# Expert numbers of the passes: packed two to a word and loaded into TensorE's registers in three loads during the routing

## The chip, the cores and the metric

One Trainium2 chip, one core, 8192 tokens of 128 floats. The time is device microseconds of one execution, and runs are compared by their median. Engines: PE is TensorE (PEld its weight loads), DVE VectorE, ACT ScalarE, POOL GpSimd, SP SyncE. Each runs its own stream of instructions, and semaphores order them.

## The reference

```
x = x + cross_attention_ffn(layernorm(x), ctx)      # BitNet linears, 2 attention layers, FFN
tokens = layernorm(x)                               # 8192 x 128
logits = tokens @ router_w.T;  top1 = argmax, p = max softmax      # 8 experts
order  = tokens of one expert by falling p; the first 1280 stay, the others go to expert 0
for e in range(8):  h = relu(tokens @ W1[e] + b1[e]);  y = h @ W2[e] + b2[e]
out = x + y of the token's own expert
```

## The kernel before, in words

The first stages compute the cross attention and its FFN for all tokens, write `x` and its norm's two numbers to rows in DRAM, and form the router's logits. None of that is touched by the change.

**Routing.** DVE and ACT find each expert's threshold digit by digit, and TensorE sums their counts. Beside this DVE builds tables: 8192 tokens sorted by expert are 64 tiles of 128 slots, and as an expert may begin inside a tile, there are `PASSES` = 71 passes, each one tile with one expert. A matmul with a matrix of ones (L1165) spreads four numbers per pass over the partitions of `psum` bank 7. DVE copies two of them as integers to one partition: `expert_of` (L1719) and `slot_of` (L1721). The semaphore `s_seg` (named segments_then_pass_tables_ready) counts these steps: 3 after `expert_of`, 4 after `slot_of`. Then TensorE ranks the tokens (L1178 to L1182), runs twelve matmuls whose result nobody reads (`keep_busy`, L963), and multiplies one-hot tables (L1189): first the 8 first tiles (`place` of `first_tile`, 64 matmuls of 16 columns), then the other 56. DVE makes these tables (L1800: rows; L1777, L1782: tiles), waits in `source(1)` (L1788) for the first product, and writes from it `src_of`, the row numbers of the tokens in each tile.

**The pass loop.** POOL gathers the rows of a tile with an indirect DMA (L640), and scatters finished tiles to the output with another (L647). In POOL's order the gathers of tiles 0 to 30 come first, then gather and scatter alternate for 33 tiles, then the last 31 scatters follow. DVE normalises a gathered tile (L1830), TensorE turns it (L1213), ACT copies it out (L872), TensorE does layer 1 (L1220, four float32 matmuls that run as eight), ACT takes the relu (L884), TensorE does layer 2 (L1229, four again), DVE adds bias and residual (L1836, L1842). SP copies the pass's layer-1 weights into one of seven buffers (L503). TensorE's order for pass a is: turn rows of a+2, layer 1 of a, layer 2 of a-2. Layer 2 addresses the resident second weights by the expert's number, in a register:

```
e = pe.value_load(expert_of[0:1, a:a + 1], min_val=0, max_val=NX - 1)
pe.wait_ge(s_hc, a + 1)
```

Of the kernel before, what the change touches and what calls it, by code (L numbers as in the profile page):

```python
# [9 lines left out]
I32 = mybir.dt.int32  # L10
I16 = mybir.dt.int16
ALU = mybir.AluOpType
# [3 lines left out]
P = 128  # L16
# [8 lines left out]
NX = 8  # L25
# [7 lines left out]
CAP = int(np.ceil(T / NX * 1.25))  # L33
TILES = T // P
PASSES = TILES + NX - 1
RING = 32
TURNS = 8
DEPTH = 4
AHEAD = 7
WP = FF + NC + E  # L40
LAG = RING - 1
FIRST = 8
# [71 lines left out]
def xattn_moe(nc, x, ctx_in, weights, biases, router_w, W1, b1, W2, b2, out):  # L114
    rows = nc.dram_tensor("token_rows", (T, XW), F32).ap()
    with ExitStack() as stack:
        def sb(name, shape, dtype=F32):
            return stack.enter_context(nc.sbuf_tensor(name, shape, dtype))
# [7 lines left out]
        ident = sb("ident", [P, P])  # L126
        ident_b = sb("ident_b", [P, P], BF16)
        ones = sb("ones", [P, P])
# [12 lines left out]
        part_no = sb("part_no", [P, 1])  # L141
# [25 lines left out]
        big = sb("big", [P, T])  # L167
# [70 lines left out]
        hT = [take_f(FF) for _ in range(DEPTH)]  # L238
        w_now = [feat[:, n * WP:(n + 1) * WP] for n in range(AHEAD)]
        src_of = sb("src_of", [P, TILES], I32)  # L240
        expert_of = sb("expert_of", [1, PASSES], I32)
        slot_of = sb("slot_of", [1, PASSES], I32)
        in_pass = sb("in_pass", [P, PASSES])
        spans = sb("spans", [P, 3, NX])
# [3 lines left out]
        by_span = sb("by_span", [P, 3, NX - 1])  # L248
        of_pass = sb("of_pass", [P, 7])
        in_low = sb("in_low", [P, PASSES])  # L250
        by_pass = big[:, 12 * 512:12 * 512 + 4 * PASSES].rearrange("p (k a) -> p k a", a=PASSES)
        cnt = sb("cnt", [P, WAYS - 1])
        reached = sb("reached", [P, WAYS - 1])
        thr_row = sb("thr_row", [NX, NX])
# [6 lines left out]
        n8 = [sb(f"n8_{n}", [P, NX]) for n in range(5)]  # L261
# [113 lines left out]
        s_seg = sem("segments_then_pass_tables_ready")  # L375
# [29 lines left out]
        def bank(n, width=512, rows_=P):  # L405
            return psum[0:rows_, n, 0:width]
# [492 lines left out]
        def _(pe):  # L899
# [60 lines left out]
            def keep_busy(n, columns):  # L960

                for _ in range(n):
                    pe.matmul(columns, f1T[:, 0, 0:P], f1T[:, 0, 0:columns.shape[-1]], start=True, stop=True)  # L963
# [120 lines left out]
            for k, (i, pair) in enumerate(pieces):  # L1084
# [4 lines left out]
                first = 4 * (i % 2) + 2 * pair  # L1089
# [70 lines left out]
            for k in range(LEVELS):  # L1160
                count_up(k, RADIX[k] - 1)
                if k + 1 < len(cuts):
                    tiles_before(cuts[k], cuts[k + 1])
            pe.wait_ge(s_seg, 2)
            pe.matmul(bank(7, 4 * PASSES), ones[:, :], by_pass.rearrange("p k a -> p (k a)"), start=True, stop=True  # L1165
                      ).then_inc(s_tab_mm, 1)
            keep_busy(3, bank(6))
            count_up(LEVELS, 4)
# [11 lines left out]
            pe.wait_ge(s_ms, 2)  # L1180
            pe.matmul(by_tile, ones_b[:, :], above_b.rearrange("p (t e) -> p t e", e=NX), start=False, stop=True)
            pe.matmul(bank(6), not_before_b[:, :], above_b, start=False, stop=True).then_inc(s_ps, 1)  # L1182
            keep_busy(12, bank(4))

            def place(dst, tiles, first, end):
# [17 lines left out]
            m.then_inc(s_inv_mm, 1)  # L1203

            pe.wait_ge(s_seg, 4)
            pe.wait_ge(s_idx, 2)
            pe.wait_ge(s_moe, 16 * 10)

# [12 lines left out]
                m.then_inc(s_l1, 1)  # L1222

            def layer2(a):
                e = pe.value_load(expert_of[0:1, a:a + 1], min_val=0, max_val=NX - 1)
                pe.wait_ge(s_hc, a + 1)
                wait(pe, s_yt, a - 1)
                for c in range(NC):
                    m = pe.matmul(bank(4 + a % 2, E), hT[a % DEPTH][:, P * c:P * c + P],  # L1229
                                  w2s[:, bass.ds(e, 1), c, :].rearrange("p e d -> p (e d)"),  # L1230
                                  start=(c == 0), stop=(c == NC - 1))
                m.then_inc(s_l2, 1)
# [13 lines left out]
        def _(dve):  # L1246
            ch = Chain(dve, s_dve)

            def do(ins):
                ch.link(ins)  # L1250
                ch.join()
# [262 lines left out]
            for k, (i, pair) in enumerate(pieces):  # L1514
                if by_vector(k):
                    dve.wait_ge(s_h, k + 1)
                    first = 4 * (i % 2) + 2 * pair
# [116 lines left out]
                                         accum_out=cnt[:, column:column + 1])  # L1634

            first, start, end = spans[:, 0, :], spans[:, 1, :], spans[:, 2, :]
            spread = bank(7, 4 * PASSES).rearrange("p (k a) -> p k a", a=PASSES)

            def pass_tables(k):

                tokens, kept, dropped, kept_to, dropped_to = (n[:, :] for n in n8)
                upto, lowest, highest, tiles_of = (n[:, :] for n in n8[0:4])
                if k == 0:
                    dve.wait_ge(s_rs_pe, 1)
                    do(dve.tensor_reduce(tokens, bank(6).rearrange("p (t e) -> p e t", e=NX), AX, ALU.add))
                elif k == 1:
                    do(dve.tensor_scalar(kept, tokens, float(CAP), None, ALU.min))
                    ch.link(dve.tensor_tensor(dropped, tokens, kept, ALU.subtract))
                    do(dve.tensor_tensor_scan(kept_to, ones[:, 0:NX], kept, 0.0, ALU.mult, ALU.add))
                elif k == 2:  # L1650
                    do(dve.tensor_tensor_scan(dropped_to, ones[:, 0:NX], dropped, 0.0, ALU.mult, ALU.add))
                    ch.link(dve.tensor_scalar(end, kept_to, dropped_to[:, NX - 1:NX], None, ALU.add))
                    ch.link(dve.tensor_scalar(start[:, 1:NX], kept_to[:, 0:NX - 1], dropped_to[:, NX - 1:NX], None,
                                              ALU.add))
                    ch.join()
                    dve.scalar_tensor_tensor(drop8[:, :], dropped_to, kept[:, 0:1], dropped, ALU.add, ALU.subtract
                                             ).then_inc(s_seg, 1)
                elif k == 3:
                    dve.wait_ge(s_seg, 1)
                    ch.link(dve.tensor_scalar(lowest, start, 0.5 - P / 2, 1.0 / P, ALU.add, ALU.mult))  # L1660
                    ch.link(dve.tensor_scalar(highest, end, P / 2 - 0.5, 1.0 / P, ALU.add, ALU.mult))
                    ch.join()
                    ch.link(dve.tensor_scalar(lowest, lowest, MAGIC, MAGIC, ALU.add, ALU.subtract))
                    do(dve.tensor_scalar(highest, highest, MAGIC, MAGIC, ALU.add, ALU.subtract))
                elif k == 4:
                    do(dve.tensor_tensor(tiles_of, highest, lowest, ALU.subtract))
                    do(dve.tensor_tensor_scan(upto, ones[:, 0:NX], tiles_of, 0.0, ALU.mult, ALU.add))
                    do(dve.tensor_tensor(first, highest, upto, ALU.subtract))
                elif k == 5:
                    ch.link(dve.tensor_tensor(span_steps[:, :, :], spans[:, :, 1:NX], spans[:, :, 0:NX - 1],  # L1670
                                              ALU.subtract))
                    do(dve.tensor_scalar(passed[:, :], upto[:, 0:NX - 1], part_no[:, :], None, ALU.is_le, ALU.add,
                                         accum_out=of_pass[:, 0:1]))
                    do(dve.tensor_tensor(by_span[:, :, :], span_steps[:, :, :],
                                         passed[:, :].unsqueeze(1).to_broadcast([P, 3, NX - 1]), ALU.mult))
                elif k == 6:
                    do(dve.tensor_reduce(span_of[:, :], by_span[:, :, :], AX, ALU.add))
                    do(dve.tensor_scalar(of_pass[:, 4:5], span_of[:, 0:1], part_no[:, :], None, ALU.add))
                    ch.link(dve.scalar_tensor_tensor(of_pass[:, 2:4], of_pass[:, 4:5].to_broadcast([P, 2]), -float(P),
                                                     span_of[:, 1:3], ALU.mult, ALU.add))  # L1680
                elif k == 7:
                    do(dve.tensor_scalar(of_pass[:, 5:6], of_pass[:, 4:5], float(TILES - 1), None, ALU.min))
                    do(dve.tensor_scalar(of_pass[:, 6:7], of_pass[:, 5:6], float(RING), -float(RING), ALU.is_ge, ALU.mult))
                    do(dve.tensor_tensor(of_pass[:, 1:2], of_pass[:, 5:6], of_pass[:, 6:7], ALU.add))
                elif k == 8:
                    dve.tensor_tensor(by_pass, ident[:, 0:PASSES].unsqueeze(1).to_broadcast([P, 4, PASSES]),
                                      of_pass[:, 0:4].unsqueeze(2).to_broadcast([P, 4, PASSES]), ALU.mult
                                      ).then_inc(s_seg, 1)

            def level(k):  # L1690
# [27 lines left out]
            dve.wait_ge(s_tab_mm, 1)  # L1718
            dve.tensor_copy(expert_of[:, :], spread[0:1, 0, :]).then_inc(s_seg, 1)  # L1719
            dve.wait_ge(s_seg, 3)  # L1720
            dve.tensor_copy(slot_of[:, :], spread[0:1, 1, :]).then_inc(s_seg, 1)  # L1721
            dve.wait_ge(s_cnt2, LEVELS + 1)
            do(dve.tensor_scalar(reached[:, 0:4], bank(1 + LEVELS % 2, 4), 0.0, None, ALU.is_ge, ALU.add,
                                 accum_out=met[:, :]))
# [87 lines left out]
            def masks():  # L1812

                ch.link(dve.tensor_tensor(n8[3][:, 0:1], part_no[:, :], end[:, 0:1], ALU.subtract))
                do(dve.tensor_scalar(in_low[:, :], spread[:, 2, :], part_no[:, :], None, ALU.is_le))
                do(dve.scalar_tensor_tensor(in_pass[:, :], spread[:, 3, :], n8[3][:, 0:1], in_low[:, :],
                                            ALU.is_gt, ALU.mult))
            where = {}

# [61 lines left out]
```

## Time and profile before

| | us |
|---|---|
| median of 3 runs | 526.41 |
| lowest, highest | 525.75, 530.26 |
| the profiled execution: its own time, which is its span | 597.2 |
| PE busy, PEld busy in it | 427.6, 348.4 |
| DVE, ACT, POOL busy in it | 368.8, 350.1, 211.0 |

The profiled execution is 70.8 us longer than the median. Its routing begins near 290 us, its first gather stands at 354.47 us, and its last scatter at 590.63 us. In rows of the timeline a start in us, a duration in us, the engine, line and operation, tiles written and read, the count, and in brackets the idle time before and what ended it. Engine names with a q at the end are sequencers.

### The profile page before, as it was taken

The page shows a single profiled execution, that of the slowest core. Times are in us where ns is not written, and L with a number is a line of the kernel's source. Part 1 is how long each engine was busy: PE and PEld are TensorE (multiplying, and loading weights), DVE is VectorE, ACT ScalarE, POOL GpSimd, SP SyncE. Part 2 cuts the span into 40 slices and gives each one's busy share as a digit, 9 for nine tenths or more (in the row PEclk, how much of TensorE's full clock was granted, in tenths as well). Part 3 has the DMA queues.
Part 4 walks back from the last instruction along what each step waited for, and adds up shares of the span by engine and source line. Part 5 has one row for each costly group of instructions (what it writes and reads, how often), then busy time and mean ns, then how long its engine had stood idle before and what let it go on. Part 6 is the DMA issues. An engine that isn't in the chain of part 4 may idle for free.

```text
span 597.2 us, 10833 instructions
## 1 busy us (share of the span) xinstructions
PE 427.6 (72%) x3058; PEld 348.4 (58%) x3058; DVE 368.8 (62%) x957; ACT 350.1 (59%) x805; POOL 211.0 (35%) x296
## 2 busy tenths in 40 slices
PE   0451348999997896898869747229777567789994
PEld 0310135898996342698537346229667566679994
DVE  3999995688887897589998893014222232334442
ACT  0679986788884795987155222126444444457762
POOL 6200571353452000001010527731555555544443
PEclk9999999999999798789775566759887988889998
DMA  9900000000000000024791312223433333445540
GB/s 197 269 20 0 1 0 2 1 2 0 0 0 2 1 1 0 1 54 92 163 261 39 132 33 49 54 74 152 141 129 125 131 124 135 143 152 189 198 165 32
DMA packets 45138, 48.69 MB, mean 82 GB/s; under 512 B 10232, under 2 KB 32800, under 8 KB 45088
## 3 DMA queue, kind: packets, MB, share of 16 engines
q1 hardware_dynamic: 39728, 38.59, 21.4%
q0 software_dynamic: 4096, 8.46, 5.4%
q10 hardware_dynamic: 1264, 1.03, 0.7%
q8 instruction: 24, 0.39, 0.3%
q14 instruction: 26, 0.21, 0.1%
HBM read 16.20 MB, written 8.45 MB: 41 GB/s over the span
## 4 chain that ended last, share of the span: by engine, by line
PE 40%; DVE 23%; ACT 12%; another core or an unknown queue 11%; issue 7%; DVEq 2%; POOL 2%; DMA 2%; SPq 0%; POOLq 0%; ACTq 0%
PE psum L1229 7%; PE psum L1220 6%; PE psum L1012 5%; PE psum L1028 4%; ACT xqT L812 2%; PE psum L1020 2%; POOL out L647 2%; DVE xqT L1830 2%; DMA keys<-in_ctx 2%; DVE xqT L1836 2%; ACT big L715 2%; DVE tok_b L1430 2%; DVE part L1404 1%; ACT tok_b L812 1%
## 5 line engine op out<-in xcount | busy, mean ns | idle before, releaser
L884 ACT ACTIVATE xqT<-psum,feat 128x128 f32<-128x128 f32 x284 | 81.2, 372 | 62.1 <-remote 30.2
L1836 DVE TENSOR_TENSOR xqT<-psum,feat 128x128 f32<-128x128 f32 x71 | 20.7, 292 | 139.8 <-remote 69.5
L647 POOL DMA_INDIRECT out<-xall,src_of x64 | 62.6, 978 | 87.1 <-DVE xall L1842 81.0
L1220 PE MATMUL psum<-xqT,feat 128*128 128x128 f32 x568 | 86.4, 302 | 9.0 <-issue 9.0
L1220 PEld LDWEIGHTS psum<-xqT,feat 128*128 128x128 f32 x568 | 80.2, 218 | 9.2 <-issue 9.2
L1229 PE MATMUL psum<-keys,xqT 128*128 x568 | 84.0, 296 | 1.0 <-issue 0.9
L1229 PEld LDWEIGHTS psum<-keys,xqT 128*128 128x128 f32 x568 | 76.2, 209 | 2.2 <-issue 0.7
L640 POOL DMA_INDIRECT xall<-token_rows,src_of x64 | 62.5, 977 | 38.5 <-issue 18.6
L1213 PE MATMUL psum<-ident,xqT 128*128 128x128 f32 x71 | 22.8, 322 | 53.8 <-DVE xqT L1830 53.3
L872 ACT COPY xqT<-psum 128x128 f32<-128x128 f32 x71 | 19.5, 275 | 58.0 <-remote 46.6
L1213 PEld LDWEIGHTS psum<-ident,xqT 128*128 128x128 f32 x71 | 11.0, 155 | 59.7 <-DVE xqT L1830 56.7
L574 POOL TENSOR_TENSOR qb<-qb,arec 128x308 f32<-128x308 f32 x32 | 21.8, 700 | 64.5 <-DVE arec L1462 64.5
L1028 PE MATMUL psum<-probT,keys 78*128 78x128 f32 x256 | 34.4, 280 | 1.8 <-ACT probT L777 1.8
L594 POOL IOTA tok_b<- 128x2048 bf16 x1 | 2.5, 2470 | 90.9 <-DVE qb L1546 90.9
L963 PE MATMUL psum<-f1T 128*128 128x512 bf16 x99 | 33.8, 493 | 0.0
L1028 PEld LDWEIGHTS psum<-probT,keys 78*128 78x128 f32 x256 | 31.3, 191 | 3.4 <-ACT probT L777 2.7
L1012 PE MATMUL psum<-keys 128*128 128x77 f32 x256 | 32.1, 277 | 1.3 <-ACT keys L662 0.9
L1012 PEld LDWEIGHTS psum<-keys 128*128 128x128 f32 x256 | 30.0, 191 | 4.3 <-ACT keys L662 1.6
L1842 DVE SCALAR_TENSOR_TENSOR xall<-xqT,in_pass,xall 128x128 f32 x71 | 25.0, 352 | 11.4 <-DVE xqT L1836 9.7
L906 PE MATMUL psum<-ident,amax 128*1 128x128 f32 x6 | 2.2, 372 | 39.9 <-DVE amax L1304 15.5
L777 ACT COPY probT<-psum 77x512 f32<-77x512 f32 x32 | 18.3, 576 | 21.0 <-PE psum L1020 21.0
L662 ACT ACTIVATE keys<-psum,bcol,scale 128x308 f32<-128x308 f32 (+1 forms) x48 | 28.3, 658 | 3.1 <-PE psum L988 2.9
(334 smaller groups left out, 1000.6 us busy)
## 6 DMA issues: line engine op xcount, KB each, us to landing
feat<-keys SPq DMA_DIRECT2D x71, 322.0 KB
token_rows<-xall SPq DMA_DIRECT2D x4, 1040.0 KB, 8.5
xall<-in_x SPq DMA_DIRECT2D x8, 512.0 KB, 7.1
keys<-in_L_ffn_W SPq DMA_DIRECT2D x1, 2048.0 KB, 14.1
keys<-in_L_ffn_W SPq DMA_DIRECT2D x8, 256.0 KB, 5.8
keys<-in_ctx SPq DMA_DIRECT2D x4, 462.0 KB, 7.3
xall<-token_rows,src_of POOLq DMA_INDIRECT x64
out<-xall,src_of POOLq DMA_INDIRECT x64
```

The source lines that it names most:

```text
L640: pool.indirect_dma_start(xring[:, t % RING, :], None, rows, bass.IndirectOffsetOnAxis(ap=src_of[:, t:t + 1], axis=0)).then_inc(s_g[t % TU ...
L647: pool.indirect_dma_start(out_rows, bass.IndirectOffsetOnAxis(ap=src_of[:, t:t + 1], axis=0), yring[:, t % RING, :], None).then_inc(s_o[t ...
L662: return act.activation(dst, src_bank, ACT.Identity, bias=bcol[:, b:b + 1], scale=scale[:, k:k + 1])
L884: m = act.activation(hT[a % DEPTH][:, P * c:P * c + P], bank(2 + a % 2)[:, P * c:P * c + P], ACT.Relu, bias=w_now[a % AHEAD][:, FF + c:FF ...
L963: pe.matmul(columns, f1T[:, 0, 0:P], f1T[:, 0, 0:columns.shape[-1]], start=True, stop=True)
L1012: m = pe.matmul(bank(1 + l)[:, CT * b:CT * b + CT], src[n % GR][:, P * b:P * b + P], kT[l][n % GR][:, CT * b:CT * b + CT], start=True, sto ...
L1028: m = pe.matmul(bank(5 + l)[:, P * b:P * b + P], ktok[l][n % (GR if l else 2)][:, P * b:P * b + P], probT[l][:, P * b:P * b + P], start=Tr ...
L1213: pe.transpose(bank(a % 2, P), gn[a % DEPTH], ident[:, :]).then_inc(s_gt, 1)
L1220: m = pe.matmul(bank(2 + a % 2)[:, P * c:P * c + P], w_now[a % AHEAD][:, P * c:P * c + P], gT[a % DEPTH], start=True, stop=True)
L1229: m = pe.matmul(bank(4 + a % 2, E), hT[a % DEPTH][:, P * c:P * c + P], w2s[:, bass.ds(e, 1), c, :].rearrange("p e d -> p (e d)"), start=(c ...
L1836: dve.tensor_tensor(yt[a % 2], bank(4 + a % 2, E), w_now[a % AHEAD][:, FF + NC:WP], ALU.add).then_inc(s_yt, 1)
L1842: dve.scalar_tensor_tensor(y, yt[a % 2], in_pass[:, a:a + 1], y, ALU.mult, ALU.add).then_inc(s_y, 1)
```

## The change

The number of passes is rounded up to 72 (`2 * PAIRS`). After `slot_of` DVE makes a third table, `pair_of`: 36 words, each 8 times the expert of an odd pass plus the expert of the even pass before it.
```diff
+PAIRS = (PASSES + 1) // 2
...
-        expert_of = sb("expert_of", [1, PASSES], I32)
+        expert_of = sb("expert_of", [1, 2 * PAIRS], I32)
+        pair_of = sb("pair_of", [1, PAIRS], I32)
...
-        by_pass = big[:, 12 * 512:12 * 512 + 4 * PASSES].rearrange("p (k a) -> p k a", a=PASSES)
+        by_pass = big[:, 12 * 512:12 * 512 + 4 * 2 * PAIRS].rearrange("p (k a) -> p k a", a=2 * PAIRS)
...
-            pe.matmul(bank(7, 4 * PASSES), ones[:, :], by_pass.rearrange("p k a -> p (k a)"), start=True, stop=True
+            pe.matmul(bank(7, 4 * 2 * PAIRS), ones[:, :], by_pass.rearrange("p k a -> p (k a)"), start=True, stop=True
...
             pe.matmul(bank(6), not_before_b[:, :], above_b, start=False, stop=True).then_inc(s_ps, 1)
+            pe.wait_ge(s_seg, 5)
+            words = []
+            for first in range(0, PAIRS, 12):
+                words.extend(nc.values_load_multi_w_load_instructions(
+                    pair_of[0:1, first:first + 12], engines=(mybir.EngineType.PE,), min_val=0, max_val=NX * NX - 1)[1])
             keep_busy(12, bank(4))
...
-            pe.wait_ge(s_seg, 4)
...
             def layer2(a):
-                e = pe.value_load(expert_of[0:1, a:a + 1], min_val=0, max_val=NX - 1)
+                e = words[a // 2] // NX if a % 2 else words[a // 2] % NX
...
-            dve.tensor_copy(slot_of[:, :], spread[0:1, 1, :]).then_inc(s_seg, 1)
+            dve.tensor_copy(slot_of[:, :], spread[0:1, 1, 0:PASSES]).then_inc(s_seg, 1)
+            dve.wait_ge(s_seg, 4)
+            dve.scalar_tensor_tensor(pair_of[:, :], spread[0:1, 0, 1::2], float(NX), expert_of[:, 0::2],
+                                     ALU.mult, ALU.add).then_inc(s_seg, 1)
...
```

TensorE in the routing, before: the last ranking matmuls, the twelve `keep_busy` matmuls (they read `f1T`) and the first of the products with the one-hot rows in `xqT`.

```order
L1181 MATMUL psum<-tok_b,ones_b 128x64x8 [waits masks_ready]
L1182 MATMUL psum<-tok_b,not_before_b 128x512
L963 MATMUL psum<-f1T 128x512 x12
L1189 MATMUL psum<-big,xqT 128x16 [waits one_hot_rows_ready,tiles_by_partition_ready,one_hot_tiles_then_tiles_by_column_ready]
L1189 MATMUL psum<-big,xqT 128x16 x15
```

The same place in the changed kernel (its lines are 2 to 7 further on; "ISA" are the register instructions and reports).

```order
L1183 MATMUL psum<-tok_b,ones_b 128x64x8 [waits masks_ready]
L1184 MATMUL psum<-tok_b,not_before_b 128x512
L1188 TENSOR_LOAD pair_of [waits segments_then_pass_tables_ready]
L1188 ISA x24
L1188 TENSOR_LOAD pair_of
L1188 ISA x24
L1188 TENSOR_LOAD pair_of
L1188 ISA x24
L965 MATMUL psum<-f1T 128x512 x12
L1196 MATMUL psum<-big,xqT 128x16 [waits one_hot_rows_ready,tiles_by_partition_ready,one_hot_tiles_then_tiles_by_column_ready]
```

Three loads and 72 register instructions now stand between the ranking and the `keep_busy` matmuls.

TensorE in the pass loop, one pass before (the layer-1 matmuls, the load, layer 2; the ISA row ahead of each layer-2 matmul works out its address):

```order
L1220 MATMUL psum<-xqT,feat 128x128 [waits hidden_relu,expert_loaded4,gatheredT_copied]
L1220 MATMUL psum<-xqT,feat 128x128 x3
L1225 TENSOR_LOAD expert_of
L1225 ISA x2
L1229 ISA [waits layer2_biased,hidden_relu]
L1229 MATMUL psum<-keys,xqT 128x128
```

The same pass in the changed kernel:

```order
L1226 MATMUL psum<-xqT,feat 128x128 [waits hidden_relu,expert_loaded4,gatheredT_copied]
L1226 MATMUL psum<-xqT,feat 128x128 x3
L1235 ISA [waits layer2_biased,hidden_relu]
L1235 MATMUL psum<-keys,xqT 128x128
```

The load and its two register instructions are gone from all 71 passes; the first address instruction of a pass holds one more operation, the remainder or quotient.

## Rows read from the trace of the kernel before

**Rows 1.** The page: engines' busy time over the whole span.
```profile
PE 427.6 (72%) x3058; PEld 348.4 (58%) x3058; DVE 368.8 (62%) x957; ACT 350.1 (59%) x805; POOL 211.0 (35%) x296
```
**Rows 2.** Waits from 365 to 597 us: us in total, times, longest.
```profile
DVE xqT L1836 <- remote: 69.5, 10, 29.8
DVE xqT L1836 <- PE psum L1229: 59.7, 33, 4.4
```
**Rows 3.** Timeline of POOL: gathers 0, 30 and two later, last scatter.
```profile
354.47 1.25 POOL L640 DMA_INDIRECT xall<-token_rows,src_of  x1 [13.62 <-DVE src_of L1790]
...
393.28 0.94 POOL L640 DMA_INDIRECT xall<-token_rows,src_of  x1 [0.30 <-issue]
...
430.66 0.97 POOL L640 DMA_INDIRECT xall<-token_rows,src_of  x1 [0.30 <-issue]
...
433.22 0.97 POOL L640 DMA_INDIRECT xall<-token_rows,src_of  x1 [0.30 <-issue]
...
590.63 0.96 POOL L647 DMA_INDIRECT out<-xall,src_of  x1 [0.30 <-DMA out<-xall,src_of]
```
**Rows 4.** Timeline of TensorE: pass 0, and two turned tiles in the loop.
```profile
366.43 1.92 PE L1220 MATMUL psum<-xqT,feat 128*128 128x128 f32 x8
...
412.07 0.27 PE L1213 MATMUL psum<-ident,xqT 128*128 128x128 f32 x1
...
413.97 0.27 PE L1213 MATMUL psum<-ident,xqT 128*128 128x128 f32 x1
```
**Rows 5.** Windows: busy us and count by engine; PEclk is the granted clock's share.
```profile
core 0: us, PE busy (x) PEld busy (x) DVE busy (x) ACT busy (x) POOL busy (x), PEclk, DMA share, GB/s
342.00:345.00 3.00, 0.75 (x4) 0.14 (x2) 2.76 (x11) 0.00 (x0) 0.00 (x0) 1.00 0.57 223
...
349.40:354.00 4.60, 4.30 (x64) 4.17 (x64) 4.57 (x6) 0.16 (x1) 0.00 (x0) 0.50 0.00 0
403.00:420.00 17.00, 16.82 (x141) 16.63 (x139) 6.91 (x21) 9.75 (x40) 3.83 (x4) 0.93 0.41 155
```
**Rows 6.** Timeline of TensorE in the routing.
```profile
339.47 3.28 PE L963 MATMUL psum<-f1T 128*128 128x512 bf16 x12
349.47 4.30 PE L1189 MATMUL psum<-big,xqT 128*128 128x16 bf16 x64 [6.72 <-DVE xqT L1800]
```
**Rows 7.** Timeline of DVE in the routing.
```profile
333.95 0.22 DVE L1721 CAST slot_of<-psum 1x71 int32<-1x71 f32 x1
334.46 0.16 DVE L1723 TENSOR_SCALAR_CACHE_REDUCE reached<-psum 128x4 f32<-128x4 f32 x1 [0.29 <-PE psum L1143]
...
348.11 4.69 DVE L1800 TENSOR_TENSOR xqT<-tok_b,row_b 128x2048 bf16<-128x2048 bf16 x5
```
**Rows 8.** Instructions of L1225: count, ns min/median/max, first and last start.
```profile
L1225 PEldq TENSOR_LOAD <-expert_of x71: 296/406/702, 369.7 to 586.8; - x71
L1225 PEldq FUSED_REGOPS  x71: 151/151/165, 370.3 to 587.2; - x71
L1225 PEldq SEQ_ASSERT  x71: 18/18/28, 370.5 to 587.4; - x71
```
**Rows 9.** The same view of L1229: the address instructions of layer 2.
```profile
L1229 PEldq FUSED_REGOPS  x284: 46/46/60, 370.6 to 587.9; - x142
```
**Rows 10.** Timeline of TensorE's weight loads in the routing.
```profile
337.68 0.23 PEld L1181 LDWEIGHTS psum<-tok_b,ones_b 128*128 128x128 bf16 x1 [0.62 <-DVE tok_b L1743]
...
339.47 0.15 PEld L963 LDWEIGHTS psum<-f1T 128*128 128x128 bf16 x1 [0.28 <-issue]
339.89 0.15 PEld L963 LDWEIGHTS psum<-f1T 128*128 128x128 bf16 x1 [0.28 <-issue]
```
**Rows 11.** Instructions of L501, and of L503 in SP's second pass: its own loads.
```profile
L501 SPq TENSOR_LOAD <-expert_of x71: 263/269/478, 334.3 to 576.8; - x71
...
L501 SPq FUSED_REGOPS  x1: 160/160/160, 336.1 to 336.1; - x1
...
L503 SPq FUSED_REGOPS  x2: 51/51/51, 336.4 to 337.6; - x2
```

More of the change, by code:

```diff
@@ L1636, in _ @@
             first, start, end = spans[:, 0, :], spans[:, 1, :], spans[:, 2, :]
-            spread = bank(7, 4 * PASSES).rearrange("p (k a) -> p k a", a=PASSES)
+            spread = bank(7, 4 * 2 * PAIRS).rearrange("p (k a) -> p k a", a=2 * PAIRS)
             def pass_tables(k):
@@ L1685, in pass_tables @@
                 elif k == 8:
-                    dve.tensor_tensor(by_pass, ident[:, 0:PASSES].unsqueeze(1).to_broadcast([P, 4, PASSES]),
-                                      of_pass[:, 0:4].unsqueeze(2).to_broadcast([P, 4, PASSES]), ALU.mult
+                    dve.tensor_tensor(by_pass, ident[:, 0:2 * PAIRS].unsqueeze(1).to_broadcast([P, 4, 2 * PAIRS]),
+                                      of_pass[:, 0:4].unsqueeze(2).to_broadcast([P, 4, 2 * PAIRS]), ALU.mult
                                       ).then_inc(s_seg, 1)
@@ L1814, in masks @@
                 ch.link(dve.tensor_tensor(n8[3][:, 0:1], part_no[:, :], end[:, 0:1], ALU.subtract))
-                do(dve.tensor_scalar(in_low[:, :], spread[:, 2, :], part_no[:, :], None, ALU.is_le))
-                do(dve.scalar_tensor_tensor(in_pass[:, :], spread[:, 3, :], n8[3][:, 0:1], in_low[:, :],
+                do(dve.tensor_scalar(in_low[:, :], spread[:, 2, 0:PASSES], part_no[:, :], None, ALU.is_le))
+                do(dve.scalar_tensor_tensor(in_pass[:, :], spread[:, 3, 0:PASSES], n8[3][:, 0:1], in_low[:, :],
                                             ALU.is_gt, ALU.mult))
```

## The prediction

> **What bounds the kernel now.** I read the waits of the last stretch first, then POOL's and TensorE's timelines in the pass loop, then the windows there, and last the routing, where the new work goes.
>
> The profiled execution lasts 597.2 us, the median of the runs is 526.41 us, so 70.8 us of the profile are not in the runs. The waits show where such time can lie: from 365 us on DVE waited 69.5 us in 10 stretches, up to 29.8 us long, for results that nothing on the page accounts for, and 59.7 us in 33 shorter ones for layer 2 [rows 2]. I therefore work out the loop twice from its undisturbed rows.
>
> POOL: gather 0 starts at 354.47, gather 30 at 393.28; the next would start 0.94 + 0.30 later, at 394.5 [rows 3]. Then a gather and a scatter together take 433.22 - 430.66 = 2.56 us, 33 times: 84.5 us, to 479.0. The last 31 scatters take 0.96 + 0.30 = 1.26 us each, so the last one starts 30 x 1.26 = 37.8 us later, at 516.8. In the profile the span ends 597.2 - 590.63 = 6.6 us after that start. POOL alone ends the kernel at 523.4 us.
>
> TensorE: pass 0 begins its layer 1 at 366.43, and an undisturbed pass takes 413.97 - 412.07 = 1.90 us [rows 4]. 71 passes are 134.9 us: 501.3, and with about 10 us for the last layer 2, its scatter and the end, 511 to 513 us.
>
> 523.4 is within 3 us of the runs' median. So I read the runs as bound by POOL's 128 indirect DMAs, one after the other from the first gather on, with TensorE some 10 us better; and even by TensorE's own count the array is full, since in 17.00 us of the loop its weight loads are busy 16.63 us [rows 5]. Either way the loop hangs on when gather 0 starts. That is set in the routing: DVE's `source(1)` needs the first product of `place`, whose 64 matmuls run from 349.47 to 353.77 [rows 6] behind DVE's hot rows (348.11 to 352.80) [rows 7].
>
> **What is removed: 71 loads in the loop.** Each was 406 ns of TensorE's sequencer, with 151 and 18 ns for the check [rows 8]. I cost their removal at nothing. The cover is the array's own work: the load stands behind layer 1's eight matmuls, and in the steady window the weight loads leave 0.37 us in 17 [rows 5], so no load opened a gap. If that cover is gone the bounds are 0 and 71 x 0.58 = 41 us, of which POOL would give back nearly nothing. The quotient or remainder adds one operation to an address instruction of 46 to 60 ns [rows 9], some 14 ns by the difference of these two, in front of the same matmuls: nothing.
>
> **What is added on DVE.** One instruction on 36 words, 0.22 us as the copy at L1721 has it, where DVE idles 0.29 us for TensorE's counts [rows 7]: 0, at most 0.2 us. The four more columns of the spreading matmul are nothing. SP and POOL issue what they issued.
>
> **What is added on TensorE's sequencer, in the routing.** This is the sum. The last ranking matmul that waits has its weights loaded at 337.68 [rows 10], and `pair_of` is ready before (its neighbours on DVE end at 334.2 [rows 7]). So the loads begin near 337.7. Before, the sequencer had from then until 349.47 nothing but twelve matmuls to issue, and the array idled 6.72 us of it [rows 6]. That is the slack: what ends before about 346 us costs nothing.
>
> Checks: 36 comparisons with their reports. 151 + 18 ns is the low bound [rows 8]; from one comparison to the next instruction SP takes 336.4 - 336.1 = 0.3 us [rows 11], the high bound. I take 0.27: 9.7 us, bounds 6.1 and 10.8.
>
> Loads: no row has a load of several words. From below it costs what a load of one word does, 0.41 us [rows 8]; from above twelve such, 4.9 us. A register operation costs 14 ns [rows 9], so a one-word load is nearly all the read. SP's shortest load, 263 ns [rows 11], less a four-operation instruction (60 ns) leaves 0.2 us for the read, and I take it that twelve reads go one after another: 0.41 + 11 x 0.20 = 2.6 us, nearer the upper end for each word than the 14 ns of a register operation. Three with 0.06 us between: 8.0 us, bounds 1.2 and 14.6.
>
> A rule of the Trainium skill speaks here, and against the change: Runtime: NRT & Kernel Launch, section Instruction fetch mechanics, says that a TENSOR_LOAD costs about 200 ns per register even in bulk, of loads from HBM. By it, as an estimate, 36 words are 7.2 us. No run here shows it yet.
>
> So the sequencer is free at 337.7 + 9.7 + 8.0 = 355.4 us, and only then issues the twelve `keep_busy` matmuls. They took 3.28 us before [rows 6], the first at 0.42 us each [rows 10]; at that price all would take 5.1, at half of it 2.6. After a longer idle I take 4.2: 359.6. Then `place`: 64 matmuls took 4.30 us with the granted clock at 0.50, the 1.2 GHz level [rows 5, 6]. Right behind `keep_busy` the granted clock was 1.00, the 2.4 GHz level, from 342 to 345 [rows 5], so I take half, 2.2 (bounds 2.15 and 4.3): 361.8. Before it was 353.77. The first product is **8.0 us late**, DVE waits for it in `source(1)` with the rest of its tables queued behind, so gather 0, the other 56 tiles' numbers and pass 0 are late by as much, and nothing later catches up. With all bounds low the end is at 347.8 and nothing is late; with all high at 372.2, 18 us late.
>
> In the profiled execution that gives 597.2 + 8.0 = 605.2 us; carried to the runs, 526.4 + 8.0 = **534.4 us**.
>
> **Rivals.**
>
> *Cheap words.* A load of twelve costs as one of one. Loads 1.4 us, sequencer free at 348.8, `place` ends at 355.2 to 357.3: 1.4 to 3.5 us late, 528 to 530 us. For it: it is one instruction and one row of memory. Against it: a one-word load is long on TensorE and on SP alike [rows 8, 11], as one trip to the memory would be. The skill's 200 ns per register speaks against it too. Chance 0.25.
>
> *Dear words.* Every word costs TensorE's whole 406 ns: 14.6 us, `place` ends at 368.4, 541 us. Loads in the loop did take up to 702 ns [rows 8]. Chance 0.13.
>
> *Nothing.* Without the profiler the sequencer takes these instructions so much faster that they end before 346 us: 526 us, and the change does nothing that counts. 36 checks and 36 words in 8 us would be 0.22 us a word with its check; the check's recorded 0.17 leaves 0.05. Chance 0.09.
>
> *Faster: the loop hung on the loads.* In the runs TensorE's sequencer, not POOL, sets the pace of a pass. 71 passes that end at 526.4 - 10 = 516 need (516 - 366.4)/71 = 2.1 us each, 0.2 more than the undisturbed 1.90, which the load and check (0.58) could well be. Freed of it the loop wins up to 14 us, of which 1.4 to 8.0 is lost in the routing: 514 to 520 us. It decides only if POOL also needs less per DMA than its rows show, else its 523.4 plus the late start stays. Against it: the full weight loads of [rows 5]. The skill's Perfetto Trace Analysis, section Identifying the Most-Contended Engine, says to work on the busiest engine first; that is TensorE with 72% [rows 1], and by that rule the change pays. But the same section judges TensorE by its weight loads, and the trace's 16.63 of 17.00 us are not the sequencer's. Chance 0.08.
>
> **How the numbers follow.** Forecast 0.45 (532 to 537 us, with checks of 0.24 to 0.30 and words of 0.15 to 0.25 us), cheap words 0.25, dear words 0.13, nothing 0.09, faster 0.08. The predicted time is the forecast's 534.4. A range from 526 to 541 holds the forecast, cheap words, half of the dear ones and half of "nothing", which scatters about the old median; it leaves out the other halves and the faster case, 0.19. 1%, 5.3 us, is what a measurement of this kernel can tell from no change. Slower by more: the forecast and dear words, 0.58. Within: cheap words and nothing, 0.34, and 0.01 of the faster rival's upper end, 0.35. Faster: 0.07.
>
> **What the changed profile would show.** Three loads on TensorE's sequencer near 338 us of 2.6 us each (0.4 for cheap words, 4.9 for dear), 36 checks 0.27 us apart, `keep_busy` from about 355 us instead of 339.47, `place` ending near 362 and the first gather near 362.5 instead of 354.47. In the loop the undisturbed pass stays at 1.90 us; if it falls, or if TensorE's weight loads had gaps in the runs that the profile lacks, the fourth rival is right. If gather 0 is late by 8 us and the time does not follow, POOL does not bound the runs, and my reading of the loop is wrong.

## The result: 1.3% slower, and the profile after

The changed kernel takes **532.82 us** (median of 12 runs, 531.59 to 536.28). The kernel before, run beside it, takes 527.04 us (12 runs). The ratio is **1.0132**, with a 95% interval of 1.0109 to 1.0155, so it is slower by more than 1%. The ratio compares fast runs alone; the plain quotient of the two medians is 1.011. Forecast were 534.4 us, in a range of 526 to 541.

The profiled execution of the changed kernel lasts 535.98 us, with a span of 534.2. The first view is the group of TensorE's sequencer instructions at the new loads, L1188: count, ns min/median/max, first and last start.

```profile
L1188 PEldq FUSED_REGOPS  x36: 146/146/165, 342.3 to 354.9; - x36
L1188 PEldq SEQ_ASSERT  x36: 18/18/28, 342.6 to 355.1; - x36
L1188 PEldq TENSOR_LOAD <-pair_of x3: 862/1441/1496, 340.8 to 350.8; - x3
```

These are the three loads and the 36 comparisons with their reports. The loads take 3.8 us together (862 + 1441 + 1496 ns), not the 8.0 of the sum. A comparison and its report are recorded as 146 + 18 ns, but between the first comparison (342.3) and the last report (355.1) lie 12.8 us. The two later loads (1496 + 862 ns) and the 0.06 us behind each of them take 2.5 of it, which leaves 10.3 us for 36 checks: 0.29 each. Only the spacing shows the price, not the recorded durations. The sequencer is busy from 340.8 to 355.1, 14.3 us.

TensorE's array in the routing (start us, us, line, operation, shapes and count, then the idle time before and what ended it):

```profile
342.33 0.71 PE L1184 MATMUL psum<-tok_b,not_before_b 128*128 128x512 bf16 x1
355.14 4.39 PE L965 MATMUL psum<-f1T 128*128 128x512 bf16 x12 [12.10 <-issue]
359.37 4.05 PE L1196 MATMUL psum<-big,xqT 128*128 128x16 bf16 x64
```

The last ranking matmul is followed by 12.10 us of nothing: the array waits for its own sequencer ("issue"). `keep_busy` comes at 355.14, and `place` right behind it. Before, `place` was the one that waited 6.72 us for DVE's hot rows [rows 6].

DVE and POOL at the same place, one fence each:

```profile
351.46 4.69 DVE L1809 TENSOR_TENSOR xqT<-tok_b,row_b 128x2048 bf16<-128x2048 bf16 x5
...
363.46 0.17 DVE L1797 COPY t<-psum 128x8 f32<-128x8 f32 x1 [6.31 <-PE psum L1196]
```

```profile
364.12 1.25 POOL L642 DMA_INDIRECT xall<-token_rows,src_of  x1 [19.88 <-DVE src_of L1799]
...
427.35 0.97 POOL L642 DMA_INDIRECT xall<-token_rows,src_of  x1 [0.30 <-issue]
428.63 0.99 POOL L649 DMA_INDIRECT out<-xall,src_of  x1 [0.30 <-issue]
429.92 0.97 POOL L642 DMA_INDIRECT xall<-token_rows,src_of  x1 [0.30 <-DVE xqT L1839]
...
527.61 0.97 POOL L649 DMA_INDIRECT out<-xall,src_of  x1 [0.30 <-DMA out<-xall,src_of]
```

DVE starts its hot rows 9.13 us after the last ranking matmul, as before (348.11 - 338.95 = 9.16 [rows 7]), then waits 6.31 us for `place`. Behind it the indirect DMAs run without a pause, a gather and a scatter in 2.57 us as before [rows 3], and the last one starts 163.5 us after gather 0. The end of the span, 534.2, lies 170.1 us behind gather 0.

**How much of it is the change.** Counted from the last ranking matmul (338.95 before, 342.33 after), gather 0 starts after 354.47 - 338.95 = 15.52 us before [rows 3] and after 364.12 - 342.33 = 21.79 us now: **6.3 us late**. The medians differ by 5.8, and by the ratio it is some 7 us, with 6.3 inside its interval. That the last ranking matmul itself comes late in this profile is nothing of the change. In an execution of the kernel before with 524.82 us (below) it starts at 337.62, 4.7 us sooner. The two executions part between 240 and 300 us, in work that is the same in both kernels, and there TensorE's granted clock differs. Of each of them (first the changed kernel, then the kernel before) the window from 250 to 260 us:

```profile
250.00:260.00 10.00, 10.00 (x68) 10.00 (x67) 6.82 (x19) 9.46 (x9) 0.00 (x0) 0.50 0.00 1
```

```profile
250.00:260.00 10.00, 10.00 (x105) 9.95 (x106) 7.87 (x22) 9.37 (x10) 0.00 (x0) 0.78 0.00 1
```

At a granted clock of 0.50 the array was full with 68 matmuls, at 0.78 with 105. Such a difference comes with both kernels: the 12 runs of the kernel before reach from 525.05 to 533.72 us, and of the changed kernel's 12 the four above 535 us have a mean granted clock of 0.887 each, the other eight 0.892 to 0.903. The two spans differ by 11.2 us: 4.7 before the routing's last matmul, 6.3 from there to gather 0, 0.2 behind it. Whoever subtracts two profiles has to split them so, and compare a median with the term in the middle.

**TensorE in the loop.** Two turned tiles of the steady stretch and the last layer 2:

```profile
426.62 0.27 PE L1219 MATMUL psum<-ident,xqT 128*128 128x128 f32 x1
...
428.51 0.27 PE L1219 MATMUL psum<-ident,xqT 128*128 128x128 f32 x1
...
508.92 2.85 PE L1235 MATMUL psum<-keys,xqT 128*128 x24
```

The pass is 1.89 us (1.90 before [rows 4]), and TensorE is done at 511.8, 16 us ahead of the last scatter's start. The waits from 365 us on have no row that answers to the 69.5 us on a "remote" result [rows 2]; DVE's wait for layer 2 is:

```profile
DVE xqT L1845 <- PE psum L1235: 51.3, 69, 3.0
```

So the profile shown of the kernel before, 597.2 us long, was one disturbed execution; one other in 29 later runs of that kernel took 620.45 us. Why was not found.

### The profile page after: what moved, and what is told of

Same layout as the page of the kernel before. It is cut to its first block, busy times and chain, and to the rows that moved or that the text cites. A ratio compares the mean times of both kernels' runs of the same rounds, so it can differ in the third digit from the quotient of the medians.

```text
span 534.2 us, 10695 instructions
## 1 busy us (share of the span) xinstructions
PE 408.4 (76%) x3058; PEld 333.5 (62%) x3058; DVE 370.7 (69%) x958; ACT 348.4 (65%) x805; POOL 211.7 (40%) x296
## 4 chain that ended last, share of the span: by engine, by line
PE 55%; DVE 18%; ACT 14%; issue 6%; DMA 3%; POOL 2%; SPq 0%; DVEq 0%; POOLq 0%; ACTq 0%
PE psum L1226 12%; PE psum L1235 12%; PE psum L1014 6%; PE psum L1030 5%; ACT xqT L814 3%; PE psum L1022 2%; DMA keys<-in_ctx 2%; ACT big L717 2%; PE psum L1118 2%; DVE part L1410 2%; ACT tok_b L814 2%; PE psum L965 2%; PE psum L1219 1%; POOL out L649 1%; ACT big L850 1%
## 5 line engine op out<-in xcount | busy, mean ns | idle before, releaser
L1226 PE MATMUL psum<-xqT,feat 128*128 128x128 f32 x568 | 76.4, 278 | 0.0
L1235 PE MATMUL psum<-keys,xqT 128*128 x568 | 74.7, 275 | 0.0
L1226 PEld LDWEIGHTS psum<-xqT,feat 128*128 128x128 f32 x568 | 70.5, 195 | 0.0
L1235 PEld LDWEIGHTS psum<-keys,xqT 128*128 128x128 f32 x568 | 69.0, 192 | 0.0
L965 PE MATMUL psum<-f1T 128*128 128x512 bf16 x99 | 36.1, 520 | 12.1 <-issue 12.1
L965 PEld LDWEIGHTS psum<-f1T 128*128 128x128 bf16 x99 | 12.3, 131 | 29.7 <-issue 27.4
L1839 DVE TENSOR_SCALAR xqT<-xall 128x128 f32 x71 | 26.5, 374 | 4.7 <-issue 3.7
```

The lines of the kernel that those rows point to most:

```text
L1226: m = pe.matmul(bank(2 + a % 2)[:, P * c:P * c + P], w_now[a % AHEAD][:, P * c:P * c + P], gT[a % DEPTH], start=True, stop=True)
L1839: dve.tensor_scalar(gn[m], xr[:, 0:E], xr[:, E:E + 1], xr[:, E + 1:E + 2], ALU.subtract, ALU.mult).then_inc(s_prep, 1)
```

## Experiments

The theory: the sequencer's loads and checks hold up `keep_busy` and `place`, gather 0 is late by what is left over the slack, and POOL carries that to the end one for one. The rivals: the loop hangs on TensorE, or on its loads.

**1. Loads without their checks.** The 36 comparisons and reports are gone, the three loads stay.

```diff
-  pair_of[0:1, first:first + 12], engines=(mybir.EngineType.PE,), min_val=0, max_val=NX * NX - 1)[1])
+  pair_of[0:1, first:first + 12], engines=(mybir.EngineType.PE,), min_val=0, max_val=NX * NX - 1,
+  skip_runtime_bounds_check_because="pairs of numbers of experts, each below NX")[1])
```

> The three loads stay where the change put them, the 36 comparisons and reports are left out. Theory (the change costs what TensorE's sequencer does in the routing beyond its slack, and the loop gains nothing): loads take 1.4 + 1.5 + 0.9 = 3.8 us as in the changed kernel's trace, the sequencer is free near 342, keep_busy ends by 346, place starts with the hot rows again; gather 0 back to 15.5 us after the last ranking matmul, 526 to 528 us, no change against the kernel before. Rival (the loop gains, and the routing eats more than it): faster than before, under 522 us. Rival (the loads, not the checks, are the cost): 530 us or more.

Measured: 526.46 us (12 runs), ratio 1.0007, interval 0.9971 to 1.0042. Its loads, `keep_busy`, `place` and first gather:

```profile
L1188 PEldq TENSOR_LOAD <-pair_of x3: 1129/1130/1409, 337.3 to 339.9; - x3
```

```profile
338.77 0.71 PE L1184 MATMUL psum<-tok_b,not_before_b 128*128 128x512 bf16 x1
341.13 2.75 PE L965 MATMUL psum<-f1T 128*128 128x512 bf16 x12 [1.64 <-issue]
349.29 4.32 PE L1197 MATMUL psum<-big,xqT 128*128 128x16 bf16 x64 [5.42 <-DVE xqT L1810]
```

```profile
354.31 1.25 POOL L642 DMA_INDIRECT xall<-token_rows,src_of  x1 [13.62 <-DVE src_of L1800]
```

The loads alone delay `keep_busy` by 1.8 us and nobody else: `place` waits 5.42 us for DVE again, and gather 0 comes 15.54 us after the last ranking matmul. Shown: with these three loads alone nothing is lost, and the loss needs the checks.

**2. Loads and checks behind `keep_busy`.** The array gets its twelve matmuls first; the same instructions then stand between them and `place`.

```diff
+            keep_busy(12, bank(4))
             pe.wait_ge(s_seg, 5)
             words = []
...
-            keep_busy(12, bank(4))
```

> Loads and checks stand behind the twelve keep_busy matmuls instead of ahead of them. Theory: the sequencer is busy until about 352 on the clock of the profile before (337.7 + 14.3), place starts there and takes 4.1 to 4.3 us, so its first product is 2.3 to 2.6 us late instead of 6.3: 529 to 530 us. Rival (what costs is keep_busy run late, not the sequencer): no cost at all, 527 us. Rival (a cold clock in place costs more than keep_busy): as slow as the change, 533 us.

Measured: 527.66 us (12 runs), ratio 1.0044, interval 1.0006 to 1.0082: somewhat less than expected. The times hardly part this from the rival of no cost (527 us); the trace does. `place` and gather 0:

```profile
351.16 4.08 PE L1196 MATMUL psum<-big,xqT 128*128 128x16 bf16 x64 [8.94 <-DVE xqT L1809]
```

```profile
355.94 1.25 POOL L642 DMA_INDIRECT xall<-token_rows,src_of  x1 [15.75 <-DVE src_of L1799]
```

The last ranking matmul of this execution starts at 338.28, so gather 0 is 17.66 us behind it, 2.1 late. The view puts `place`'s wait down to DVE, but what ended last was the sequencer's last check, at 351.0. The other 4.1 us of the 6.3 are the twelve `keep_busy` matmuls, which in the changed kernel stand behind the checks and take 4.23 us to `place`.

**3. The loop keeps its loads, and the routing gets the new ones too.** The new registers are filled and not used.

```diff
-                e = words[a // 2] // NX if a % 2 else words[a // 2] % NX
+                e = pe.value_load(expert_of[0:1, a:a + 1], min_val=0, max_val=NX - 1)
```

> The routing's loads and checks as in the change, their words unused: the loop loads one word per pass again, as before. Theory (removing the loop's loads is worth nothing): the same time as the changed kernel, 532 to 534 us. Rival (the loop gains by the removal, which pays back part of the routing's cost): slower than the change by that gain, 537 us or more.

Measured: 534.61 us (6 runs), ratio 1.0149, interval 1.0092 to 1.0206, which holds the changed kernel's 1.0132. Removing 71 loads from the loop is worth nothing that shows. The times alone would leave room for some 3 us; the profile is narrower, since its span ends 170.0 us behind gather 0 with the loads in the loop (536.4 - 366.41) and 170.1 without them. On TensorE the removal is worth a little: from the first layer 1 to the end of the last layer 2 it needs 138.7 us here, 139.2 in the kernel before (experiment 5), and 135.9 in the changed kernel. POOL's order of DMAs covers these 3 us. The other profiles agree: 138.7 us in experiment 6, which also has the loads, and 136.0 to 136.8 in the eight others without them.

**4. Loads and checks right ahead of the pass loop,** behind all of the routing's matmuls. The same lines, moved.

> Loads and checks stand behind the last product of the routing, right ahead of the pass loop: gather 0 is as early as before, and TensorE begins the loop 14.3 us later. Theory (POOL's 128 DMAs set the end, TensorE has room): scatter 0, which POOL reaches 40 us after gather 0, now waits 3 to 5 us for pass 7, and that alone is lost: 530 to 532 us. Rival (TensorE sets the pace): all 14 us are lost, 541 us. Rival (POOL never waits): 527 us.

Measured: 525.88 us (12 runs), ratio 0.9984, interval 0.9951 to 1.0018: no cost; the expected 530 to 532 fell, and the rival stated with it holds. Gather 0, the first layer 1 and the last scatter:

```profile
353.59 1.25 POOL L642 DMA_INDIRECT xall<-token_rows,src_of  x1 [13.61 <-DVE src_of L1799]
...
517.38 0.97 POOL L649 DMA_INDIRECT out<-xall,src_of  x1 [0.30 <-DMA out<-xall,src_of]
```

```profile
373.99 1.94 PE L1226 MATMUL psum<-xqT,feat 128*128 128x128 f32 x8
```

Layer 1 of pass 0 starts 20.4 us behind gather 0 (373.99 - 353.59), where experiment 1 has 11.9 (366.21 - 354.31). TensorE is 8.5 us late with the whole loop and ends its last layer 2 at 510.0, still 7.4 us ahead of the last scatter, and the kernel is not slower: the clearest sign that TensorE does not end it, and that only what is ahead of gather 0 counts.

**5. The kernel before, profiled again.**

> The kernel before, unchanged, profiled once more. Theory (the 70 us of waits in the profile shown belong to that one execution): gather 0 near 354, the last scatter 163 to 164 us behind it, the span ends 170 us behind gather 0 at 523 to 525 us; TensorE takes 1.90 us per pass with its loads in the loop, and ends its last layer 2 ten us or more before the last scatter. Rival (the loads do set the pace of a pass): a pass takes 2.0 to 2.1 us and TensorE ends within 8 us of the last scatter.

Measured: 524.82 us, span 523.0. First and last indirect DMA, and the turned tiles of three passes:

```profile
353.15 1.25 POOL L640 DMA_INDIRECT xall<-token_rows,src_of  x1 [13.61 <-DVE src_of L1790]
...
516.43 0.97 POOL L647 DMA_INDIRECT out<-xall,src_of  x1 [0.30 <-DMA out<-xall,src_of]
```

```profile
422.97 0.27 PE L1213 MATMUL psum<-ident,xqT 128*128 128x128 f32 x1
425.08 0.27 PE L1213 MATMUL psum<-ident,xqT 128*128 128x128 f32 x1
426.98 0.27 PE L1213 MATMUL psum<-ident,xqT 128*128 128x128 f32 x1
```

The last scatter starts 163.3 us after gather 0 and the span ends 169.8 after it, as in the changed kernel. TensorE ends its last layer 2 at 504.0, 12.4 us ahead of the last scatter, so the rival falls. Most passes take 1.90 us. One of these two took 2.11: with the loads in the loop a pass is held up now and then. Of 61 passes in the middle of the loop 9 take over 1.95 us here (1.5 us too much in all), 13 in experiment 3 (2.5 us) and none in the changed kernel, so a good part of the 3 us of experiment 3 lies there.

**6. The kernel before without its last eight scatters.**

```diff
-                if t >= LAG:
+                if LAG <= t < TILES + LAG - TURNS:
...
-                pool.wait_ge(s_o[n], 16 * (TILES // TURNS))
+                pool.wait_ge(s_o[n], 16 * (TILES // TURNS - 1))
```

> The kernel before without the scatters of the last eight tiles, so that these tiles' rows of the output are not written; all passes and gathers stay. Theory (POOL's indirect DMAs, one after the other, end the kernel): 8 scatters x 1.27 us = 10 us less, 516 us. Rival (TensorE's passes end it): the scatters lie beside them and only the last one's tail counts, 524 us or more.

Measured: 515.16 us (4 runs), ratio 0.9838, interval 0.977 to 0.9906; 10.2 us less than 525.32, where 8 x 1.27 was expected. TensorE's last layer 2 ends at 505.2, 138.7 us after the first layer 1, so TensorE did the same work in the same time. Its last indirect DMA:

```profile
508.02 0.97 POOL L647 DMA_INDIRECT out<-xall,src_of  x1 [0.31 <-DMA out<-xall,src_of]
```

Shown: POOL's DMAs end this kernel, and a scatter taken away at the end gives its full 1.27 us.

**7. What a load of several words costs.** The changed kernel without comparisons, its 36 words in 36, 9, 6 or 2 loads; each has only the numbers 12 changed in the loop over `first`.

> The changed kernel with 36 loads of one word in place of three of twelve, and without the comparisons. Theory (a load has a fixed part, and a further word costs some 0.07 us): each takes what a load of one word took in the loop of the kernel before, 0.30 to 0.41 us, with 0.06 between 13 to 17 us in all; keep_busy starts 13 to 17 us behind the start of the first load, and gather 0 comes 8 to 11 us later than in the kernel before, counted from the last ranking matmul: 23 to 27 us instead of 15.5. Rival (what a load costs here does not go by its words: six words took 1.6 us in the mean, twelve 1.2): 1.2 to 1.6 us each, 45 us or more in all, and a time above 550 us.

> The changed kernel with nine loads of four words, and without the comparisons. Theory (fixed part and a small price by word): 0.5 to 0.7 us each, 5 to 7 us in all. Rival (1.2 to 1.6 us a load, whatever its words): 11 to 15 us in all.

> The changed kernel with six loads of six words in place of three of twelve, and without the comparisons. Theory (a load has a fixed part near 0.3 us and a word costs 0.07 to 0.1 us): 0.7 to 0.9 us each, 4.2 to 5.4 us in all against 3.7 for three of twelve without comparisons. Rival (a load costs one trip whatever its words): 1.1 to 1.4 us each, 7 to 8 us in all. Rival (only words count): 0.55 to 0.7 us each, the same 3.7 us in all. The time stays at 526 us in each case but the second, where the loads end near 346 us and it still does within 1 us.

> Six loads of six words, without the comparisons, once more: whether the two loads of 2.2 and 2.5 us belong to the kernel or to that execution. If to the kernel, the second and the fourth are again above 2 us and all six take 9 to 10 us; if to the execution, 0.8 to 1.4 us each, 5 to 8 us in all.

> The changed kernel with two loads of eighteen words, and without the comparisons. Theory (fixed part and a small price by word): 1.5 to 1.8 us each, 3.0 to 3.6 us in all. Rival (1.2 to 1.6 us a load, whatever its words): 2.4 to 3.2 us in all. In both cases the time is that of the kernel before, since the sequencer is free before DVE's hot rows are there.

The loads, one fence for each kernel, in that order:

```profile
L1188 PEldq TENSOR_LOAD <-pair_of x36: 294/305/852, 337.3 to 352.7; - x36
```

```profile
L1188 PEldq TENSOR_LOAD <-pair_of x9: 327/424/888, 337.6 to 342.4; - x9
```

```profile
L1188 PEldq TENSOR_LOAD <-pair_of x6: 813/1428/2526, 344.5 to 353.0; - x6
```

```profile
L1188 PEldq TENSOR_LOAD <-pair_of x6: 817/1427/2500, 336.3 to 344.7; - x6
```

```profile
L1188 PEldq TENSOR_LOAD <-pair_of x2: 2656/4452/6248, 336.0 to 338.7; - x2
```

With the single runs' times, and gather 0 counted from the last ranking matmul (15.52 us in the kernel before):

| words a load | all loads, from the first start to the last end | `keep_busy` after the last ranking matmul | gather 0 after it | time |
|---|---|---|---|---|
| 1 | 15.7 us | 14.27 us | 23.69 us | 534.73 us |
| 4 | 5.1 us | 3.70 us | 15.51 us | 526.42 us |
| 6 | 9.9, 9.9 us | 8.50, 8.47 us | 18.13, 17.69 us | 535.94, 527.24 us |
| 12 (experiment 1) | 3.8 us | 2.36 us | 15.54 us | 526.46 us (median) |
| 18 | 9.0 us | 7.53 us | 16.96 us | 526.11 us |

What a load costs goes with what else runs at the time. In the kernel with one word a load the first 14 loads stand where the 16 DMA engines are busy (mean share 0.65), the last 22 where they are silent. The loads, then all engines, before and after 345 us:

```profile
L1188 PEldq TENSOR_LOAD <-pair_of x14: 300/508/852, 337.3 to 344.5; - x14
L1188 PEldq TENSOR_LOAD <-pair_of x22: 294/302/310, 345.1 to 352.7; - x22
```

```profile
337.20:345.00 7.80, 2.29 (x4) 0.39 (x2) 6.50 (x17) 2.99 (x1) 3.17 (x6) 0.72 0.65 255
345.00:353.00 8.00, 0.00 (x0) 0.00 (x0) 7.76 (x18) 0.72 (x1) 0.00 (x0) 0.50 0.00 0
```

One word takes 0.30 us in the quiet stretch and 0.51 in the median of the other. DVE is busy in both. That the DMA traffic makes the difference is likely, but no experiment here took it away. A load of four words, in a stretch as busy (0.68), took no longer than a load of one: 0.42 us in the median. Of the changed kernel's loads of twelve the first two (1.44 and 1.50 us) have DMA beside them and the third (0.86) has none; against 0.30 for one word that is 0.05 for each further word.

One and four words came out about as expected (15.7 and 5.1 us in all); six and eighteen agree with neither theory. Six words cost more than twelve in the median, and their last load took 1.47 us with no DMA beside it. One load of eighteen took 6.2 us, and that kernel's gather 0 is 1.4 us late, where no delay was expected. The two kernels with six words agree load by load, the second and the fourth above 2.1 us in both, so it belongs to the program and not to the execution. What makes these widths dear stays open; no run here separates the width from the address at which a load begins. The 535.94 us of the first of them is a late routing (its last ranking matmul starts at 346.03, the other's at 337.80), not its loads, which cost the same in both.

The table answers another question better than it was asked. `keep_busy` up to 3.7 us after the last ranking matmul costs nothing; at 7.53 gather 0 is 1.4 us late, at 8.47 2.2, at 14.27 8.2. The changed kernel itself has 12.81 and 6.3 us. The difference of the two, 5.9 to 6.5 us, is the slack, and beyond it every microsecond of the sequencer counts in full.

## Why the prediction was right

The sign, the mechanism and its size hold; that the size fits so well is in part luck, as the sum below shows. Point by point, by the prediction's own steps:

- **POOL bounds the runs; the end is tied to gather 0.** Shown three ways: the span ends 169.8 to 170.4 us behind gather 0 in all eleven undisturbed profiles of the kernels with all scatters; eight scatters less give 10.2 us; and a TensorE 8.5 us later costs nothing. It was put at 523.4 - 354.5 = 168.9 us.
- **The 71 removed loads are worth nothing.** Shown by experiment 3. The reason given, that no load opened a gap in the array, was a little off: some loads did hold a pass up, and TensorE does gain 3 us over the loop, under POOL's cover.
- **Checks, 9.7 us.** Measured 10.3 (0.29 us each instead of 0.27). The sum was right to go by SP's spacing [rows 11] and not by the recorded 169 ns [rows 8].
- **Loads, 8.0 us: mis-sized.** They take 3.8. The step that failed is "twelve reads go one after another" at 0.2 us each, taken from SP's shortest load less a register instruction. That a one-word load is long says how long one trip is, not what the next word costs: with no DMA beside it, 0.30 us for one word and 0.86 for twelve leave 0.05 for each further word. The rule of the Trainium skill that was weighed there (Runtime: NRT & Kernel Launch, Instruction fetch mechanics: about 200 ns per register even in bulk) is stated for loads from HBM; by it, as an estimate, the loads would have taken 7.2 us. The runs disagree for twelve words (862 to 1496 ns, 72 to 125 a word) and, in the median, for four (106 a word), while eighteen took up to 347 ns a word.
- **`keep_busy`, 4.2 us.** Measured 4.39 to its end, 4.23 to `place`.
- **`place`, 2.2 us: mis-sized.** It takes 4.05. The step that failed is "so I take half", at the other level of the clock: these matmuls do not go by the clock. In the changed kernel the granted clock is 1.00 (the 2.4 GHz level) when `place` begins behind the `keep_busy` matmuls, and 0.50 (1.2 GHz) when it ends. All of it, then half a microsecond at either level:

```profile
359.40:363.40 4.00, 4.00 (x65) 3.93 (x63) 0.00 (x0) 0.00 (x0) 0.00 (x0) 0.81 0.02 4
360.90:361.40 0.50, 0.50 (x12) 0.50 (x11) 0.00 (x0) 0.00 (x0) 0.00 (x0) 1.00 0.00 0
361.90:362.40 0.50, 0.50 (x12) 0.50 (x11) 0.00 (x0) 0.00 (x0) 0.00 (x0) 0.50 0.00 0
```

As many matmuls and weight loads run at 0.50 as at 1.00, one of each every 62 ns or so. The window of before had a hint: weight loads busy 4.17 us of 4.60, 64 of them [rows 5]. Whether the weight load sets the 62 ns or the handing out of the instructions does, no run here separates. Nor were the 4.30 us of before all work: their matmuls start 61 to 62 ns apart too, but for two pauses of together 0.23 us, at the 17th and the 33rd matmul, where `place` waits for the next of DVE's five hot-row instructions. All six profiles in which the first of these released `place` have both pauses, the seven others neither; in the changed kernel the hot rows end 3 us before `place` starts.

- **The sum.** Loads 4.2 us too much, `place` 1.85 too little, checks 0.6 too little: net 1.75 too much, and 8.0 became 6.3. Two wrong sizes cancelled in part; the bounds kept for both held them. With 6.3 the sum would have said 532.7. The forecast's own condition, 0.15 to 0.25 us a word, did not come true: twelve words took 0.07 to 0.125 us each. The two sums of all bounds are a little off in the prediction: its low terms give 349.8 us and not 347.8, its high ones 372.5 and not 372.2; nothing hangs on it.

Of the rivals, *cheap words* was nearer on the loads (3.8 us against its 1.4 and the forecast's 8.0), but its 528 to 530 us are below every one of the 12 runs. *Nothing* is refuted by the time, whose interval begins at 1.0109, and *dear words* by the L1188 rows: 14.3 us of sequencer work, 3.8 of it loads. *Faster* is refuted by experiments 3 and 4.

No version tried here beats the kernel before: loads without checks, or loads ahead of the pass loop, bring the changed kernel back to it and no further, since the loop's gain is TensorE's alone.

## What to carry to other kernels

Find what the end is tied to (here the start of the first of 128 transfers in a row), and ask of every edit only whether it moves that start. Work moved out of a loop in which it was covered is paid where it lands: here a stretch with some 6 us of slack got sequencer work that held the array up for 12.8 us, and the same instructions a few lines further down were free. Price sequencer instructions by the spacing of their neighbours, since the recorded durations of these checks are little over half of it, and before you halve a time by the clock, look whether the same matmuls have run at both levels, and how far apart.

## What was not expected of the hardware

- A load of one word into TensorE's registers takes 0.30 us (294 to 310 ns, 22 loads) while the DMA engines are silent, and 0.51 in the median (up to 0.85, 14 loads) while they are busy at a share of 0.65, in one execution.
- A load of several words goes neither by its words nor by the number of loads: medians of 0.42 us for four, 1.13 for twelve without comparisons, but 1.43 for six (up to 2.5) and 2.7 and 6.2 for eighteen, repeated load by load in two executions of the six.
- A comparison with its report is recorded as 164 ns and takes 0.29 us of the sequencer.
- The matmuls of 16 columns start some 62 ns apart at a granted clock of 1.00 and of 0.50 alike: 12 of them in half a microsecond, with 11 weight loads, at both.
- Ahead of the routing's last matmul, in work that is the same in both kernels, two executions differ by 4.7 us, with a granted clock of 0.50 in the one and 0.78 in the other between 250 and 260 us; the runs of the kernel before spread over 8.7 us.
